# A hybrid transformer block on one core: waits between GpSimd operations, and a new table of places for the side work

## The reference, cut to what matters

```
x = x + attention(layernorm(x))     # RMS norm xn, q, k, v, 16 heads of 16, causal softmax; returns xn + out
x = x + ffn(layernorm(x))           # base matmul + low rank (shared + 6 routed of rank 16, top 2 of 6)
x = x + ssm(layernorm(x))           # causal conv of 4 taps, silu, then for each of 16 states n:
                                    #   decay = exp(A[:, n] * dt);  inp = dt * xc * B[n]
                                    #   h = decay * h + inp  over 512 steps;  y += h * C[n]
                                    # result: (y * sigmoid gate) @ Wo
x = x + ffn(layernorm(x))           # the same ffn and weights again
```

## Time and profile before

| | us |
|---|---|
| three runs: median (lowest to highest) | 2261.72 (2260.11 to 2261.73) |
| the profiled execution: its own time | 2251.14 |
| its span, first to last instruction | 2249.3 |
| PE, DVE, ACT, POOL busy | 1831.8, 1769.5, 1398.9, 1164.6 |
| mean granted TensorE clock | 0.925 |

### The profile page before, as it was taken

The page is one execution under the profiler, slowest core; times in us unless marked ns, Lnnn a source line. Parts: engine busy times, 40 slices in busy tenths (PEclk is TensorE's granted clock), DMA queues, the critical chain, the costliest instruction groups (busy, mean ns, idle before and its releaser), DMA issues.

```text
span 2249.3 us, 32508 instructions
## 1 busy us (share of the span) xinstructions
PE 1831.8 (81%) x10881; PEld 1093.5 (49%) x10912; DVE 1769.5 (79%) x2568; ACT 1398.9 (62%) x2692; POOL 1164.6 (52%) x1042
## 2 busy tenths in 40 slices
PE   5789797888879787788988888887988888877775
PEld 2445454545455554545555454544545454535333
DVE  5434688888798887979888898979788796968684
ACT  2456667576766757666775767676575766574531
POOL 1001565645465654646565464646555474646582
PEclk8989799999999999989999999999999999989887
DMA  4212576656667675755757666666767565551110
GB/s 113 82 56 67 118 153 138 149 129 135 128 138 163 135 151 123 148 122 133 158 130 151 138 145 142 132 129 134 157 137 152 124 146 122 123 123 52 49 60 14
DMA packets 186055, 275.58 MB, mean 123 GB/s; under 512 B 33553, under 2 KB 125730, under 8 KB 185890
## 3 DMA queue, kind: packets, MB, share of 16 engines
q1 hardware_dynamic: 155650, 163.40, 28.8%
q0 software_dynamic: 30240, 110.11, 26.3%
HBM read 128.72 MB, written 34.08 MB: 72 GB/s over the span
## 4 chain that ended last, share of the span: by engine, by line
PE 35%; DVE 20%; ACT 16%; DMA 13%; issue 8%; SPq 4%; POOL 3%; ACTq 0%; POOLq 0%; DVEq 0%
PE bank L315 6%; DMA sk<-qk_parts 6%; DVE hc L1114 6%; PE bank L505 5%; PE bank L324 3%; SPq L700 3%; PE bank L359 3%; ACT dec L878 3%; PE bank L407 3%; DVE hc L1121 3%; PE bank L488 3%; DMA sq<-qk_parts 3%; ACT pt L769 3%; PE bank L382 2%; DVE diff L1063 2%
## 5 line engine op out<-in xcount | busy, mean ns | idle before, releaser
L1286 POOL TENSOR_TENSOR inp<-u,b_all 128x512 f32<-128x512 f32 x512 | 720.1, 1440 | 410.0 <-DVE hc L1114 302.9
L1114 DVE TENSOR_TENSOR_SCAN hc<-dec,inp 128x1024 f32<-128x1024 f32 x256 | 630.9, 2464 | 32.9 <-ACT dec L878 31.3
L769 ACT ACTIVATE pt<-bank 128x512 f32<-128x512 f32 x640 | 375.6, 595 | 248.6 <-PE bank L384 243.0
L359 PE MATMUL bank<-sk,sq 96*128 96x512 bf16 (+3 forms) x1024 | 282.2, 314 | 183.8 <-DMA sk<-qk_parts 80.7
L878 ACT ACTIVATE dec<-dt,a_neg 128x511 f32<-128x511 f32 x512 | 337.7, 715 | 35.0 <-DVE hc L1114 34.9
L1121 DVE TENSOR_TENSOR hc<-hc,bank 128x1024 f32<-128x1024 f32 x242 | 293.7, 1214 | 74.4 <-PE bank L544 72.6
L1293 POOL DMA_DIRECT2D y<-hc x210 | 185.6, 884 | 281.0 <-DVE hc L1121 99.7
L382 PE MATMUL bank<-sq,sk 98*128 98x512 bf16 (+3 forms) x1024 | 281.3, 313 | 21.4 <-ACT pt L769 14.9
L359 PEld LDWEIGHTS bank<-sk,sq 96*128 96x128 bf16 x1024 | 102.9, 100 | 331.0 <-DMA sk<-qk_parts 86.9
L993 DVE TENSOR_REDUCE mall<-bank 128x1 f32<-128x512 f32 x256 | 172.4, 674 | 109.7 <-PE bank L361 109.6
L995 DVE TENSOR_REDUCE mall<-bank 128x4 f32<-128x512 f32 x256 | 173.2, 677 | 60.4 <-PE bank L361 60.3
(11 more groups left out here) (160 smaller groups left out, 3401.5 us busy)
## 6 DMA issues: line engine op xcount, KB each, us to landing
y<-hc POOLq DMA_DIRECT2D x210, 512.0 KB, 5.1
b_all<-b_kept SPq DMA_DIRECT2D x256, 256.0 KB, 4.2
qk_parts<-parts SPq DMA_DIRECT2D x96, 256.0 KB, 2.9
sq<-qk_parts SPq DMA_DIRECT2D x384, 64.0 KB, 3.5
sk<-qk_parts SPq DMA_DIRECT2D x384, 64.0 KB, 3.6
X<-in_x SPq DMA_DIRECT2D x16, 512.0 KB, 6.6
out<-X SPq DMA_DIRECT2D x16, 512.0 KB, 3.0
sq<-hlt SPq DMA_DIRECT2D x256, 2.0 KB
```

The lines of the kernel that those rows point to most:

```text
L359: mm(dst[:, o:o + n], sq[0:KS, slot, h, qb * P:(qb + 1) * P], sk[0:KS, slot, h, 0:n], start=True, stop=False)
L769: A(pt[:, n % PT, :], score_bank[unit % 2][:, :], ACT.Exp).then_inc(exp_done.sem, 1)
L1114: V.tensor_tensor_scan(h, d, v, 0.0, ALU.mult, ALU.add).then_inc(scan_done.sem, 1)
L1286: last = G.tensor_tensor(inp[:, n % 2, c, :], u[:, c, :], b_all[:, k % 3, :], ALU.mult)
```

## The change

Two edits. First, a list `ended` in the POOL stream holds the signal of each data operation's end; `behind()` waits for the last one, and is put before the first operation of `rsqrt`, `weigh_low`, `weigh`, `residual` and `inputs`. Inside `weigh`, `residual` and `inputs` each operation now signals and the next waits for it. DMAs issued by POOL are neither waited for nor made to wait. Second, the tables of places, some banks and `FINISH` are new.

```diff
+            ended = []
+            def behind():
+                if ended:
+                    pool.wait_ge(*ended[-1])
+            def ends(signal, b, n=None):
+                ended.append((signal.sem, signal.at(b, n)))
 def weigh(a):                       # residual: likewise, one wait between its two additions
-                for tb in range(TB):
-                    last = G.tensor_tensor(tok_q[:, tb, :], tok_q[:, tb, :], w_row[:, :], ALU.mult)
-                last.then_inc(weighed.sem, 1)
+                behind()
+                for tb in range(TB - 1):
+                    G.tensor_tensor(tok_q[:, tb, :], tok_q[:, tb, :], w_row[:, :], ALU.mult).then_inc(pool_own.sem, 1)
+                    pool.wait_ge(pool_own.sem, pool_own.one())
+                G.tensor_tensor(tok_q[:, TB - 1, :], tok_q[:, TB - 1, :], w_row[:, :], ALU.mult).then_inc(weighed.sem, 1)
+                ends(weighed, a)
 def inputs(s, n):
-                for c in range(C):
-                    last = G.tensor_tensor(inp[:, n % 2, c, :], u[:, c, :], b_all[:, k % 3, :], ALU.mult)
-                last.then_inc(inp_ready.sem, 1)
+                behind()
+                G.tensor_tensor(inp[:, n % 2, 0, :], u[:, 0, :], b_all[:, k % 3, :], ALU.mult).then_inc(pool_own.sem, 1)
+                pool.wait_ge(pool_own.sem, pool_own.one())
+                G.tensor_tensor(inp[:, n % 2, 1, :], u[:, 1, :], b_all[:, k % 3, :], ALU.mult).then_inc(inp_ready.sem, 1)
+                ends(inp_ready, s, n + 1)
```

More of the change, by code:

```diff
@@ L105, in hybrid_block @@
     ACT_AT = {"square_f": 98, "square_s": 125, "square_l": 252, "norm_q": -94, "norm_f": 103, "exp0": 116,
-              "norm_s": 132, "softplus": 152, "decays": 160, "norm_l": 257, "exp1": 266, "xn": (-77, -71),
[3 rows of a table removed]
+              "norm_s": 132, "softplus": 153, "decays": 160, "norm_l": 257, "exp1": 266, "xn": (-77, -71),
[3 rows of a table added]
               "low1": 264, "hw1": 275}
-    DVE_AT = {"add_x1": (94, 96), "in0": 109, "out0": 116, "add_up0": (124, 124), "silu": 143, "delta": 155,
-              "gated": 246, "add_x3": (251, 251), "in1": 265, "out1": 266, "add_up1": (277, 280), "stats_q": -100}
-    POOL_AT = {"weigh": -56, "residual": -45, "rsqrt_f": 97, "rsqrt_s": 122, "rsqrt_q": -102, "inputs": 153,
+    DVE_AT = {"add_x1": (94, 96), "in0": 113, "out0": 116, "add_up0": (123, 123), "silu": 143, "delta": 155,
+              "gated": 246, "add_x3": (251, 251), "in1": 265, "out1": 266, "add_up1": (277, 280), "stats_q": -99}
+    POOL_AT = {"weigh": -57, "residual": -45, "rsqrt_f": 100, "rsqrt_s": 122, "rsqrt_q": -102, "inputs": 151,
                "rsqrt_l": 254, "low": (111, 266)}
-    SP_AT = {"parts": (-42, -3), "load_x": -112, "store_b": 146, "store": 278}
-    FINISH = 13
+    SP_AT = {"parts": (-43, -4), "load_x": -115, "store_b": 152, "store": 279}
+    FINISH = 14
     HEADS_PE, HEADS_DVE = 4, 4
@@ L1255, in rsqrt @@
                 G.tensor_tensor(nm[:, kind, :], ng[:, kind, :], rs[:, kind, :], ALU.mult).then_inc(scaled[kind].sem, 1)
+                ends(scaled[kind], b)
             def weigh_low(b, f):
+                behind()
                 pool.wait_ge(wts_done[f].sem, wts_done[f].at(b))
@@ L1263, in weigh_low @@
                                 ALU.mult).then_inc(hw_done[f].sem, 1)
+                ends(hw_done[f], b)
             def weigh(a):
@@ L1267, in weigh @@
                     pool.wait_ge(side["xn", c].full, side["xn", c].at("xn", a, c))
-                for tb in range(TB):
-                    last = G.tensor_tensor(tok_q[:, tb, :], tok_q[:, tb, :], w_row[:, :], ALU.mult)
-                last.then_inc(weighed.sem, 1)
+                behind()
+                for tb in range(TB - 1):
[3 more added lines that the diff above has]
+                ends(weighed, a)
             def residual(a):
                 pool.wait_ge(weighed.sem, weighed.at(a))
[L1274 to L1277, removed]
+                behind()
+                first, second = (X[:, a % XS, 2 * j:2 * j + 2, :] for j in range(2))
+                G.tensor_tensor(first, first, tok_q[:, 0:2, :], ALU.add).then_inc(pool_own.sem, 1)
+                pool.wait_ge(pool_own.sem, pool_own.one())
+                G.tensor_tensor(second, second, tok_q[:, 2:, :], ALU.add).then_inc(res_done.sem, 1)
+                ends(res_done, a)
             def inputs(s, n):
```

4 lines of the change are left out of this document (2 added, 2 removed), and 10 rows, old and new, of tables (ACT_AT, PE_AT).

## The result

The changed kernel takes 2201.86 us (median of four runs, 2186.46 to 2208.57) against 2261.72 (2260.11 to 2265.48): ratio 0.972, 95% interval 0.967 to 0.978. Four more runs of it, beside others of the kernel before, gave 2202.48 and 0.976 (0.972 to 0.979). The forecast was 2238 with a range of 2205 to 2264: the direction is right, the size is not, and the time lies outside the range.

What follows compares the result with a forecast made beforehand. No engine bounds the kernel; the chain hops between PE, DVE, ACT and DMAs, with 13 router stalls. -21.6 (router) - 10 (ssm start) + 3 (last ssm) = -28.6, cut to -24: 2261.7 - 24 = 2238 us, range 2205 to 2264.

Steps and rivals of the forecast that it cites:

- The mechanism at the router: Waits between POOL operations let DVE's router operations in: five one-operation holds replace one of six; DVE gains 1.9 us per stall.
- I take 1.8: Gain on the path per router stall from the POOL waits, in us; over 12 stalls, 21.6 us.
- upper bound, 4.4: Most one router stall could gain, in us: the router held once, by one POOL operation of 1.0, then POOL free.
- The start of an ssm: Moves on ACT and PE bring bc_low earlier: net 0.9 us a frame, taken as 0.8 in 13 frames, 10 us.
- Cost 0: in0 and FINISH 14 make second- and third-group stacked maxima 0.65 and 1.7 us later, within slack of 1.7 and 2.3.
- taken as 0: add_up0, stats_q, x1's bank and ao's second half on PE: between -0.3 and 0.3 us a frame each, counted as nothing.
- The sixth taken back for paths that come up next: Allowance on the whole sum: -28.6 us reduced to -24 for other paths that become the longest.
- The last ssm: POOL has no idle time there, so waits cost 0.11 to 0.3 us a step: 2 to 6 us, taken as 3.
- scans wait for inp: Listed sign of a wrong forecast: DVE's scans waiting for POOL's inputs; no size given.
- Rival 3: Router no longer meets weigh, or only once: 53 us gained instead of 21.6, 2202 in all; chance 0.10.
- Rival 1: POOL-DVE port does not open, or PE and DMAs eat the gain: 2255, or 2258 with terms halved; chance 0.20.
- rival 2: Stacked maxima become late in second and third groups: 49 us added, 2282; chance 0.15 with other slowdowns.

Runs made afterwards that it cites:

- the two halves: Kernel before with all waits between POOL operations, old positions: 2225.31 us, ratio 0.984; kernel before with all new positions, no new wait: 2228.31 us, 0.986.
- the run with bc early: Kernel before with softplus and the middle part of bc one slot later on ACT and PE, no new wait: 2233.02 us, ratio 0.988.
- the two fillers: Kernel before with eight, then four, unread multiplications added on PE in its wait for bc_low: 2265.23 us (1.001) and 2268.23 us (1.004).
- changed, bc put back: Changed kernel with bc, softplus and dt put back to their old positions: 2233.37 us, ratio 0.988 to the kernel before.
- the eight fillers of the first kernel: Kernel before with eight unread multiplications of 128x512 added on PE in its wait for bc_low: 2265.23 us, ratio 1.001.
- the four of the second: Kernel before with four unread multiplications of 128x512 added on PE in its wait for bc_low: 2268.23 us, ratio 1.004.

## Why the prediction was wrong

The terms of the sum, set against the two halves: the forecast had 21.6 - 3 = 18.6 us for the waits and 10 for the positions, and measured were 36.5 and 33.5. It took back 4.8 us for the two together, and measured were 10. So 18 us are missing at the waits and 23.5 at the positions, and 5 go off again: the 36 us by which the forecast fell short.

- **The mechanism at the router was right, its size was not.** The step that failed is "PE behind it waits 1.59 us for the maximum, so PE gains at least 1.6" and, from it, "I take 1.8". I read one wait of PE. A second one follows about 2 us later, there and in the frame of the earlier trace rows, which is shown here, and both are gone in the changed kernel:

```profile
1308.80 0.38 PE L359 MATMUL bank<-sk,sq 96*128 96x512 bf16 x1 [1.59 <-DVE mall L995]
1310.92 0.34 PE L359 MATMUL bank<-sk,sq 96*128 96x384 bf16 x1 [0.70 <-DVE mall L990]
```

1.59 + 0.70 = 2.3, and 2.1 to 2.5 were measured in frames at full clock. In 13 frames that is 27 to 33 us. Part of the rest of the 36.5 lies in the frames in which the clock fell in this stretch, fewer with the waits (5 and 7 of 11 before, 4 and 0 with waits); the forecast had no term for them. Its upper bound, 4.4, held.
- **The start of an ssm: 22 to 31 us and not 10.** The step that failed is "Net 0.9 us per frame ... I take 0.8 on the path". As to the cast it was about right: PE's wait is 1.4 us shorter, less some 0.5 for dt, if dt costs anything. What was left out is the clock, 1.0 us a frame in the run with bc early. The row with 3.44 us for four multiplications stood in the earlier trace rows, beside rows of 1.88 for the same four; I read the wait ahead of it and not the duration. The window view showed 0.56 there. The Trainium skill says in "TensorE: Matmul & The Clock Gate", "Part 1", that the clock follows PE's recent activity and halves after idle time; the trace agrees, and the forecast should have weighed it.
- **The moves on DVE: 11 us and not 0.** I checked that the stacked maxima would not become late, which was nearly right (3 us in sum), and the steps that failed are "Cost 0" (in0 and FINISH) and "taken as 0" (add_up0 and stats_q): no gain was weighed. I didn't ask which wait lies behind them: PE's for the stacked parts, 80.7 us in the trace of before, the largest sum of all. With these moves PE comes to it 1.0 us later, the DMA ends it no later, and the clock falls behind it in 7 of 11 frames and not in all.
- **The sixth taken back for paths that come up next**, 4.8 us, was an allowance without rows behind it. The parts lose 10 of 70 us where they meet, a seventh, but within their intervals: it is neither shown nor refuted.
- **The last ssm** was right: forecast 3 us slower, and its sixteen steps take 3.3 to 3.6 us more, in the way that was named for the upper bound: the scan slips in ahead. The sign "scans wait for inp", listed as one of being wrong, is there, in the last ssm.
- **Rival 3** gave 2202, near the measured time by another mechanism, which is luck: the router still meets weigh in every frame. Rival 1 is refuted by the waits alone, rival 2 (49 us of waits for the stacked maxima) by a sum of 8.4 us of them (second trace 9.3), where before had 5.2 (6.6).
- **The skill's rule** that I weighed ("SBUF — State Buffer", "Who interferes with whom") lets the loser wait for one instruction. After a wait, the trace agrees (1.23 us); for operations back to back it does not: an operation of DVE that meets weigh and inputs took 5.0 to 6.1 us in 11 or 12 frames of each of the nine traces in which both were there without waits, 3.60 behind weigh_low and weigh, and 2.9 to 3.1 behind two of inputs. "GPSIMD Engine Reference", "Instruction dispatch", says that consecutive instructions are no barrier between the engine's cores; the starts before the end of the one ahead agree with that. That this is why the port stays taken is argued, not shown.

## What to carry to other kernels

Where POOL runs several data operations back to back, try a semaphore wait between them if DVE has operations with two SBUF inputs in that time; three waits a frame gave 1.6% here, and moving the run elsewhere gave nothing. Where POOL and DVE alone set the pace, waits cost: 0.35 us a step in the last ssm. When a wait on PE is shortened, read the durations behind it as well as the wait, and add up all the waits behind the delay, not the first. Filling PE's idle time with dead work gave nothing at the two places tried; shortening the wait did.

## What the runs showed of the hardware

TensorE's clock after one idle time of PE, by the duration of the same four multiplications (128x512, fp32) behind it:

```
PE idle before them     traces                      frames at full clock throughout
0 to 0.8 us             the two fillers             26 of 26
2.4 to 3.1 us           eleven with the new bc      75 of 154
3.3 to 3.8 us (*)       changed, bc put back         0 of 14
4.3 to 4.5 us           six with the old bc          0 of 84
```

(*) Then one subtraction, and at most 0.3 us idle again. With the eight fillers of the first kernel the four multiplications followed without idle time, with the four of the second after 0.75 us.

In the second row the same idle time gave either level in the same kernel (3 to 11 of 14 frames), so two traces of one kernel differ in it. Frames come in lengths some 3 us apart (in the changed kernel's first trace five of 122.5 to 123.3 us and six of 125.8 to 126.9), and the runs of most kernels spread over 10 to 30 us: the changed one from 2186 to 2217, waits only no more than 3. With that, a difference of 0.3% between two such kernels needs more than four runs.
